# A graph attention, graph convolution and LSTM kernel: statistics, row maximum, weight splitting and two gates change their places

## The reference

```python
h = jnp.maximum(_layernorm(x), 0.0)
x = x + _L0_gnn_ref(h, adj, W, a)
h = jnp.maximum(_layernorm(x), 0.0)
x = x + _L1_gnn_ref(h, adj, Wg0, bg0, Wg1, bg1, Wih, Whh, bih, bhh)
```

## Time and profile before

| what | us |
|---|---|
| median of 3 runs (lowest to highest) | 462.44 (461.45 to 463.85) |
| the profiled execution's own time | 464.01 |
| its span in the trace | 462.2 |
| TensorE, VectorE, ScalarE, GpSimd busy | 433.5, 379.4, 322.9, 77.6 |
| mean granted clock of TensorE, as a share of full speed | 0.978 |

### The profile page before, as it was taken

The page is one execution under the profiler, slowest core; times in us unless marked ns, Lnnn a source line. Parts: engine busy times, 40 slices in busy tenths (PEclk is TensorE's granted clock), DMA queues, the critical chain, the costliest instruction groups (busy, mean ns, idle before and its releaser), DMA issues.

```text
span 462.2 us, 8017 instructions
## 1 busy us (share of the span) xinstructions
PE 433.5 (94%) x2550; PEld 380.9 (82%) x2550; DVE 379.4 (82%) x976; ACT 322.9 (70%) x632; POOL 77.6 (17%) x182
## 2 busy tenths in 40 slices
PE   6579999979998999999999999999999999999991
PEld 5358888879997999999878888899999988887881
DVE  3799999986779878788777888888788788888895
ACT  3479999966787678887676676767667675564550
POOL 5758841230419100000000000000000000000000
PEclk9689999989999999999999999999999999999998
DMA  8910000000000000000000000000000000002116
GB/s 244 333 41 1 2 2 1 0 0 1 1 3 1 0 0 0 0 0 1 0 0 2 0 2 0 0 1 2 0 1 1 1 1 1 0 23 69 45 48 182
DMA packets 14075, 11.68 MB, mean 25 GB/s; under 512 B 982, under 2 KB 12252, under 8 KB 13788
## 3 DMA queue, kind: packets, MB, share of 16 engines
q1 hardware_dynamic: 11404, 9.97, 7.1%
q10 hardware_dynamic: 2640, 1.33, 1.1%
HBM read 7.10 MB, written 4.19 MB: 24 GB/s over the span
## 4 chain that ended last, share of the span: by engine, by line
PE 69%; DVE 18%; ACT 4%; issue 3%; DMA 3%; DVEq 1%; SPq 1%; ACTq 0%
PE ps L967 47%; PE ps L1089 11%; PE ps L1093 6%; DVE score L699 4%; DVE score L665 3%; DMA xs<-in_x 3%; DVE xs L713 3%; DVE stats L655 2%; PE ps L947 2%; ACT v_norm L491 1%; ACT work L596 1%; DVE xs L848 1%; PE ps L1011 1%; ACT prob L524 1%; PE ps L1007 1%
## 5 line engine op out<-in xcount | busy, mean ns | idle before, releaser
L596 ACT ACTIVATE work<-ps,bl 128x512 f32<-128x512 f32 (+2 forms) x204 | 111.2, 628 | 30.8 <-PE ps L1093 23.4
L967 PE MATMUL ps<-h_hi,wl_hi 128*128 128x512 f32 (+3 forms) x252 | 94.5, 375 | 4.0 <-DVE h_lo L759 3.2
L967 PE MATMUL ps<-h_lo,wl_hi 128*128 128x512 f32 (+3 forms) x252 | 93.9, 372 | 0.0
L967 PE MATMUL ps<-h_hi,wl_lo 128*128 128x512 f32 (+3 forms) x252 | 93.8, 372 | 0.0
L586 ACT ACTIVATE work<-work 128x512 f32<-128x512 f32 (+2 forms) x56 | 31.5, 570 | 44.3 <-DVE work L843 33.6
L967 PEld LDWEIGHTS ps<-h_hi,wl_hi 128*128 128x128 f32 x252 | 47.5, 188 | 11.5 <-issue 3.2
L967 PEld LDWEIGHTS ps<-h_lo,wl_hi 128*128 128x128 f32 x252 | 47.6, 189 | 7.5
L491 ACT ACTIVATE v_norm<-xs,shift,scale 128x128 f32 (+1 forms) x128 | 52.6, 489 | 1.1 <-POOL shift L393 1.0
L967 PEld LDWEIGHTS ps<-h_hi,wl_lo 128*128 128x128 f32 x252 | 47.6, 189 | 6.5
L1089 PE MATMUL ps<-s_hi,wl_hi 128*128 128x512 f32 (+2 forms) x144 | 51.9, 362 | 0.0
L1089 PE MATMUL ps<-s_hi,wl_lo 128*128 128x512 f32 (+2 forms) x144 | 51.4, 359 | 0.0
(11 more groups left out here) (131 smaller groups left out, 968.7 us busy)
## 6 DMA issues: line engine op xcount, KB each, us to landing
result<-xs SPq DMA_DIRECT2D x12, 256.0 KB, 2.3
work<-in_w_ih_t SPq DMA_DIRECT2D x1, 1024.0 KB, 10.0
work<-in_w_hh_t SPq DMA_DIRECT2D x1, 1024.0 KB, 8.7
xs<-in_x SPq DMA_DIRECT2D x2, 256.0 KB, 3.7
xs<-in_x SPq DMA_DIRECT2D x1, 512.0 KB, 7.0
result<-xs SPq DMA_DIRECT2D x4, 128.0 KB, 3.4
result<-xs ACTq DMA_DIRECT2D x4, 128.0 KB, 3.7
adj_raw<-in_adj ACTq DMA_DIRECT2D x1, 256.0 KB, 7.5
```

Source lines behind the costliest of these rows:

```text
L596: nc.scalar.activation(lw[:, par, g, 0:cols], ps[:, 4 * par + g, 0:cols], ACT.Tanh if g == G else ACT.Sigmoid, bias=bl[:, (p - 1) * GATES ...
L967: ins = nc.tensor.matmul(dst, a, b, start=start and n_ == 0, stop=stop and n_ == 2)
```

## The change

- VectorE: the statistics of groups 3 to 5 (from tile 16 on) follow in turns 1 to 6, eight at the end of each. The first statistic of the second layer norm stands at the start of a turn ahead of the wait for S, the second behind that wait ahead of the scores; none stand between the scores and z any more. low and ebias are taken in the same turn as the scores, between and behind the z instructions. The second layer's statistics count on a semaphore of their own, `stats_x1`.
- ScalarE: waits for each pair's scale; the second layer's normalisation of pair 0 stands in turn 16 of phase_a, ahead of the copy pT.
- TensorE: 28 instead of 16 idle transposes; gates I and G of the first round's half 0 move into phase_b, turn 20, ahead of its wait for the last convolution.
- GpSimd: the twelve weight pieces wait for `one_lo` of 1, 1, 2, 3, 4, 4, 5, 6, 7, 7, 8 and 9; every subtraction is waited for; `wl_ok` counts the first weights and then all of them.

```diff
@@ GpSimd
-            def split_weights(p, m):
+            def split_weights(p, m, c):
                 i, j = (p - 1) // 2, (p - 1) % 2
-                for c in range(2):
-                    g = slice(c * 2 * D, (c + 1) * 2 * D)
-                    done(nc.gpsimd.tensor_copy(wl_of[0][i][:, j, m, g], wraw[:, m, p - 1, g]))
-                    ins = nc.gpsimd.tensor_tensor(wl_of[1][i][:, j, m, g], wraw[:, m, p - 1, g],
-                                                  wl_of[0][i][:, j, m, g].bitcast(fp32), ALU.subtract)
-                ins.then_inc(wl_ok, 1)
+                g = slice(c * 2 * D, (c + 1) * 2 * D)
+                done(nc.gpsimd.tensor_copy(wl_of[0][i][:, j, m, g], wraw[:, m, p - 1, g]))
+                done(nc.gpsimd.tensor_tensor(wl_of[1][i][:, j, m, g], wraw[:, m, p - 1, g],
+                                             wl_of[0][i][:, j, m, g].bitcast(fp32), ALU.subtract))
...
             pool.wait_ge(lstm_w_in, 32)
-            split_weights(1, 0)
-            pool.wait_ge(wl_ok, 1)
+            split_weights(1, 0, 0)
+            split_weights(1, 0, 1)
+            nc.gpsimd.nop().then_inc(wl_ok, 1)
 
             for c in range(4):
-                pool.wait_ge(stats_ok, TILES + (c + 1) * QUARTER)
+                pool.wait_ge(stats_x1, (c + 1) * QUARTER)
                 norm_scale(1, c * QUARTER, QUARTER)
 
-            pool.wait_ge(one_lo, 1)
-            for n_, (p, m) in enumerate((p, m) for p in range(2, SKIPS + 1) for m in range(2)):
-                split_weights(p, m)
-                pool.wait_ge(wl_ok, n_ + 2)
+            for n_, (p, m, c) in enumerate((p, m, c) for p in range(2, SKIPS + 1) for m in range(2) for c in range(2)):
+                pool.wait_ge(one_lo, 1 + 3 * n_ // 4)
+                split_weights(p, m, c)
+            nc.gpsimd.nop().then_inc(wl_ok, 1)
@@ ScalarE
                 if live(0):
-                    if isinstance(t, int):
-                        act.wait_ge(ln_ok, t + 1 if t < 7 else PAIRS)
+                    act.wait_ge(ln_ok, t + 1)
...
+            def second_norm(t):
+                act.wait_ge(ln_ok, t + (PAIRS + 1))
+                normalise(1, t, range(4), b_v)
+
             def phase_a(t, ph, live):
                 behind = (t - 1, ph - 1, lambda s: live(s + 1))
                 early_a(*behind)
                 first_norm(t, ph, live)
+                if isinstance(t, int) and t == PAIRS:
+                    act.wait_ge(a_T, PAIRS)
+                    second_norm(0)
                 late_a(*behind)
...
-                if live(0):
-                    after(act, b_lo[0], t, 0)
-                    if isinstance(t, int) and t == 0:
-                        act.wait_ge(a_T, PAIRS)
-                    act.wait_ge(ln_ok, t + (PAIRS + 1))
-                    normalise(1, t, range(4), b_v)
+                if live(0) and not (isinstance(t, int) and t == 0):
+
+                    act.wait_ge(b_lo[0], t)
+                    second_norm(t)
...
-            act.wait_ge(wl_ok, 2 * SKIPS - 1)
+            act.wait_ge(wl_ok, 2)
@@ VectorE
-            first_statistics(FIRST, 0)
-            first_statistics(FIRST, 1)
...
-                                           ).then_inc(stats_ok, 1)
-
-                for k in range(0):
-                    statistics(k)
-
+                                           ).then_inc(stats_x1, 1)
+
+                statistics(0)
...
                 def row_maximum(k):
 
-                    m = (ph - 2) % 4
+                    m = (ph - 1) % 4
                     if k == 0:
...
-                    elif k == 1:
-                        dve.wait_ge(low_ok, t - 1)
+                    elif k == 3:
+                        dve.wait_ge(low_ok, t)
...
                     dve.wait_ge(a_S, t)
-                for k in range(4):
-                    if live(2):
-                        row_maximum(k)
-                    if live(1):
+                statistics(1)
+                if live(1):
+                    for k in range(4):
                         ins = scores(k)
-                if live(1):
                     ins.then_inc(a_t, 1)
-                for k in range(0, 2):
-                    statistics(k)
                 if live(1):
 
                     dve.wait_ge(a_wh, t)
...
-                    ins.then_inc(a_z, 1)
+                        if k == 3:
+                            ins.then_inc(a_z, 1)
+                        row_maximum(k)
...
-                if isinstance(t, int) and t < 4:
-                    first_statistics(FIRST + 1 + t // 2, t % 2)
+                if isinstance(t, int) and 1 <= t < 7:
+                    first_statistics(FIRST + (t - 1) // 2, (t - 1) % 2)
@@ TensorE
-            turns(16)
+            turns(28)
...
+            def gate_of_window(r, k, par, g, stop):
+
+                v = (window_cols(h_hi, r, par, k), window_cols(h_lo, r, par, k))
+                return product(like_window(ps[:, 4 * par + g, :], r, par), weights(steps_of(r), 0, g), v, True, stop)
+
             def phase_b(t, ph, live):
                 if live(5):
...
+                    if isinstance(t, int) and t == PAIRS + 4:
+
+                        pe.wait_ge(wl_ok, 2)
+                        for s in range(1, 4):
+                            pe.wait_ge(b_lo[s], PAIRS)
+                        pe.wait_ge(one_lo, 4)
+                        for g in (I, G):
+                            gate_of_window(0, 0, 0, g, True).then_inc(c_gate[0], 1)
                     pe.wait_ge(b_lo[4], t - 4)
...
-                    pe.wait_ge(wl_ok, 2 * SKIPS - 1)
+                    pe.wait_ge(wl_ok, 2)
...
                         for g in gates:
+                            if (r, k, par) == (0, 0, 0) and g in (I, G):
+                                continue
```

More of the change, by code:

```diff
@@ L181, in preln_gat_gcn_lstm_kernel @@
         stats_ok = sem("stats_ok")
+        stats_x1 = sem("stats_x1")
         ln_ok = sem("ln_ok")
@@ L971, in parts, with weights @@
                 return s_hi[:, s, :], s_lo[:, s, :]
+            def weights(p, m, g):
+                c = slice(g * D, (g + 1) * D)
+                return wl(0, p, m)[:, c], wl(1, p, m)[:, c]
+            def gate_of_window(r, k, par, g, stop):
+                v = (window_cols(h_hi, r, par, k), window_cols(h_lo, r, par, k))
+                return product(like_window(ps[:, 4 * par + g, :], r, par), weights(steps_of(r), 0, g), v, True, stop)
             def phase_b(t, ph, live):
@@ L1027, in _ @@
             ticks(pe, 6, 1, phase_b, first=BESIDE)
-            def weights(p, m, g):
-                c = slice(g * D, (g + 1) * D)
-                return wl(0, p, m)[:, c], wl(1, p, m)[:, c]
             def transpose_pair(q):
@@ L1063, in _ @@
                         a_n = acts_before(r, k) - 1
-                        v = (window_cols(h_hi, r, par, k), window_cols(h_lo, r, par, k))
                         for g in gates:
+                            if (r, k, par) == (0, 0, 0) and g in (I, G):
+                                continue
                             if g in seen and (r, k) != (0, 0):
@@ L1071, in _ @@
                                 pe.wait_ge(d_out, 2 * k + par)
-                            ins = product(like_window(ps[:, 4 * par + g, :], r, par), weights(p, 0, g), v, True, k == 0)
+                            ins = gate_of_window(r, k, par, g, k == 0)
                             if k == 0:
```

## The result

The changed kernel takes 473.79 us (median of 4 runs, 472.48 to 475.66), the kernel before on the same chip 462.35 (461.45 to 463.85): a ratio of 1.0239, 95% interval 1.0210 to 1.0267, 11.4 us slower. The forecast was 472.1 (466 to 477). The profiled execution took 475.03 us, one of the upper two of the four (472.48, 472.56, 475.03, 475.66); its span is 473.2, 11.0 more than the profiled span of before, at a mean granted clock of 0.973 (0.978 before).

What follows compares the result with a forecast made beforehand. VectorE was taken to bound the attention stage, mostly TensorE from the convolutions on. Terms 11.6 + 2.7 - 3.6 - 1.0 = +9.7 gave 472.1 us on the median (473.7 for the profiled execution), range 466 to 477.

Steps and rivals of the forecast that it cites:

- (a): Fill of the attention stage, up to turn 7's scores: TensorE waits for adjT_ok behind later statistics, +11.6 us (+10 to +13).
- Rival 1: Fill: the wait for adjT costs nothing, VectorE alone sets the fill; 460.6 us, or 457.3; chance 0.12.
- (f): Waiting for each pair's scale, two counters and nops: nothing, as scales are done ahead while TensorE still stands.
- (b): Nine steady attention turns: VectorE's waits on itself lose their cover, 0.3 a turn, +2.7 us (0 to 3.6).
- Rival 2: The adjT wait stands but VectorE's waits on itself cost nothing, in steady turns and turns 5, 6: 468.8 us; chance 0.16.
- (c): End of the attention stage: earlier normalisation of pair 0 and earlier ebias are off the path, 0 (1.27 either side).
- (d): Convolutions: LSTM weight pieces spread out no longer disturb a VectorE turn, -3.6 us (-1.5 to -3.6).
- (e): TensorE's gap ahead of the last one-step LSTM gates, filled by two moved gates: -1.0 us (0 to -1.4).
- Rival 3: Convolutions: weight pieces still meet VectorE's SBUF instructions, so spreading them yields nothing: 475.7 us; chance 0.06.
- rival 4: Last one-step gates: the two moved gates don't fill the gap, held by weights or banks: 473.1 us; chance 0.06.

Runs made afterwards that it cites:

- the early split: Changed kernel, but GpSimd splits the transposed adjacency ahead of its wait for the fourth group's statistics: 466.16 us, ratio 1.0067.
- after: The changed kernel itself, all parts of the change applied to the kernel before: 473.79 us, ratio 1.0239.
- the early scale: Changed kernel with the adjacency split early and eight of the fourth group's 16 statistics ahead of the first scores: 462.94 us, ratio 1.0008.

## Why the prediction was right, and where it was off

(a) Right in mechanism and size. The stop for adjT_ok, its length (32.07 for "about 32"), the half clock behind it and the third scores (36.74 for 36.3) came as worked out from the queue orders; the early split shows that this wait held the third pair, the old place of the statistics that they are its cause. Rival 1 needed adjT_ok by 21.5 and got it at 31.92. That the sum came out within 0.1 (11.53 for 11.6) is partly luck: the third scores were 0.4 late, and the turns behind them were 0.5 shorter than forecast. What the forecast didn't say is that a second wait lay under the first: in (f) the scale of the fourth group was "nothing", because TensorE would still stand. That holds only beside the wait for adjT_ok; with it gone, the scale costs 3.2 us by the medians (466.16 against 462.94).

(b) The step that failed, in size. The forecast had 0.3 a turn, 2.7 in all; it was 4.27, outside its bound of 3.6. Of its two parts, the 0.2 between scores and z is right as a gap (0.19 in the trace), though an instruction put into it gave back only about 0.1 a turn. The other, "I take 0.1" for the statistics behind the additions, is about right for instructions alone: nine written-out turns cost 3.02, and an undisturbed one takes 5.29 for 4.97 before. In turns 5 and 6 of the fill, where eight statistics of 1.55 us stand behind the additions, a turn takes 6.7 and not 5.29 + 1.55 = 6.84, so that gap can be covered too. What was left out is the loop. In it, each statistic has register work that was hidden while other instructions were in flight ahead of it, and isn't any more: 1.25 to 1.7 us in nine turns, shown by the loop written out, and in the chain by the pieces marked DVEq. Rival 2, that VectorE's waits on itself cost nothing, falls with the run that restores the old order: 4.97 us come back in its trace. The Trainium skill (VectorE: DVE Perf Modes, The DRAIN you can't avoid) says of eight copies in a row that a semaphore behind each costs nothing extra; no run here has such a chain. Here an instruction waits for an accumulator read, and the trace has 0.19 for it; the runs don't tell the cost of the semaphore from that of the result.

(c) 0, measured -0.12 in the traces; the run with the old place of the normalisation shows nothing that stands out of the spread.

(d) and (e) Right: -3.58 and -1.03 in the traces, -3.6 and -1.1 as changes of their own. Rival 3 and rival 4 fall with that. Two pieces at most run at a time, and the VectorE instruction that the earlier trace rows show disturbed, with two inputs in SBUF (L767 now), takes 0.69 in all 16 turns.

The sum was 9.7 and is 11.0 in the profiled executions, 11.4 on the medians. The difference is (b).

## What to carry to other kernels

Before work is moved behind an earlier start, follow the waits of everything queued behind its consumer: here 16 short statistics stood two queues away from the row sums, and behind that wait lay another, which only showed once the first was gone. When a run falls between two explanations, look at how usual its profiled execution is before its trace is used as a price. On an engine that is the bound, keep an independent instruction between one that writes a value and the next one that reads it: the order of a full list of instructions was worth 0.3 to 0.45 us a turn here, with no instruction added. And a part of a change that pays should be tried without the rest: pieces and gates gained 4.6 us, hidden by a loss of 15.8.

## What the runs showed of the hardware

**Register work shows when an engine runs dry.** The same kind of register work stands in the loop of before, where an undisturbed turn takes 4.96 to 5.02 with VectorE busy throughout, and the last turn but one written out ahead of it took 4.96 (44.97 to 49.93): nothing shows. In the changed kernel, where an instruction waits for the engine's own last one, it does: 5.43 us a turn in the loop, 5.29 written out. At the loop's entry and wrap the turn was 5.70.

**The same idle transposes don't always keep the clock.** The 28 take 5.82 us in the profile of after and end at 11.40, right ahead of the first real transposes; in the run with the early split (first scores 15.03) and in the one with the old normalisation the same 28 took 3.25. TensorE then waited 1.66 us for its first tiles (1.43 in the second), and its granted clock from 13 to 15 us was 0.50 (0.51). Two rows of TensorE's timeline in the run with the early split:

```profile
5.19 3.25 PE L898 MATMUL ps<-ident 128*128 128x128 f32 x28
10.10 0.63 PE L934 MATMUL ps<-ident,v_norm 128*128 128x128 f32 x4 [1.66 <-ACT v_norm L491]
```

and the window of that run, columns as above:

```profile
13.00:15.00 2.00, 2.00 (x5) 0.86 (x5) 0.00 (x0) 0.79 (x2) 1.91 (x4) 0.50 1.05 290
```

The rows point to the clock. Eight transposes of the same shape later in after take 1.03 us at a granted clock of 1.00 and 1.79 at 0.50 (timeline of TensorE):

```profile
112.37 1.03 PE L957 MATMUL ps<-ident,prob 128*128 128x128 f32 x8
...
118.56 1.79 PE L957 MATMUL ps<-ident,prob 128*128 128x128 f32 x8
```

That is 0.13 and 0.22 us each; the 28 took 0.12 each where they were fast and 0.21 each in after. By this estimate they ran at the upper level in the two executions that then lost it, and at the lower in after, though the granted clock of both profiles is 1.00 there. That the record misses the lower level at the start is not shown directly; in the run of the pieces alone it has 1.00 from 13 to 15 us too, while S takes 1.91 (13.82). What separates the executions is the wait ahead of the first tiles: in the six profiles with one (1.06 to 3.03 us; before, pieces, gates, 16 transposes and the two named here) the first S takes 1.79 to 1.91, in the seven without one 1.02. And the time that a given number of transposes fills is not the same in each execution. The Trainium skill (TensorE: Matmul & The Clock Gate, Part 1) says that the point where the clock comes up varies from run to run of one kernel; the pace of the 28 agrees, with 3.25 to 5.82 us for the same list.

**GpSimd beside a tiny VectorE instruction.** The run with the early scale has two turns of 6.1 us. In the first, which also enters the loop (5.70 without a disturbance), ebias (two inputs in SBUF, 128x4) takes 0.57, where it takes 0.15 otherwise, and it ends when a subtraction of GpSimd does; in the second it takes 0.68 and low 0.32 beside GpSimd's casts. The timeline of VectorE in that run:

```profile
51.02 0.57 DVE L678 SCALAR_TENSOR_TENSOR ebias<-m,low 128x4 f32<-128x4 f32 x1
```

and that of GpSimd:

```profile
50.85 0.72 POOL L412 TENSOR_TENSOR rs_parts<-rs_raw,rs_full 32x256 fp32r<-32x256 f32 x1
```

It is the damage of the earlier trace rows again, at 0.4 us for an instruction that moves next to nothing, and it can be 1.0 us: ebias took 1.22 in the run with 16 transposes and 1.20 in that with the early split. Both times it began 0.51 behind the start of six casts of adjP and ended within 0.1 of their end. Running beside such casts is not enough, though: in the changed kernel's profiled execution the same ebias began 0.51 behind the same casts (81.28 and 80.77) and took 0.15. What decides between the two isn't shown. The Trainium skill (SBUF — State Buffer, Who interferes with whom) says that a Vector instruction with two SBUF inputs contends with GpSimd's reads, and this agrees.
